# The conditioning product of a two-layer kernel in 64-row tiles of the array, in place of a block-diagonal matrix

## The reference, cut to what matters

```
x = x + L0_ffn(L0_cond(x))      # L0_cond: out[b,d,t] = sum_c x[b,c,t] * W[cond[b]][c,d], W is 64 x 64
x = x + L1_ffn(L1_cond(x))
```

## Time and profile before

| | us |
|---|---|
| runs | 2144.24, 2148.28, 2148.89 (median 2148.28) |
| span of the profiled execution | 2146.3 |
| TensorE matmul busy | 2024.6 (94%) |
| TensorE weight load busy | 1896.7 (88%) |
| VectorE busy | 1691.0 (79%) |
| GpSimd busy | 554.9 (26%) |
| ScalarE busy | 488.7 (23%) |
| L947 matmuls (conditioning product) | 1024, median 275 ns |
| L964 / L965 / L966 matmuls | 1536 each, mean 342 / 341 / 341 ns |

### The profile page before, as it was taken

The page is one execution under the profiler, slowest core; times in us unless marked ns, Lnnn a source line. Parts: engine busy times, 40 slices in busy tenths (PEclk is TensorE's granted clock), DMA queues, the critical chain, the costliest instruction groups (busy, mean ns, idle before and its releaser), DMA issues.

```text
span 2146.3 us, 37287 instructions
## 1 busy us (share of the span) xinstructions
PE 2024.6 (94%) x11969; PEld 1896.7 (88%) x12032; DVE 1691.0 (79%) x4631; ACT 488.7 (23%) x1312; POOL 554.9 (26%) x470
## 2 busy tenths in 40 slices
PE   7989899999999999999999999999999999999997
PEld 6989899999999999999988788878887888888885
DVE  6898886555555555555579999999999999999999
ACT  3111111111111111111123322232223222322232
POOL 3644311111111111111123232233223332323222
PEclk9999999999999999999999999999999999999999
DMA  7754433233233332332444444444444444444442
GB/s 241 239 154 134 124 115 115 90 109 101 90 112 98 98 111 90 110 100 90 145 126 134 134 125 148 133 134 125 149 132 125 134 129 148 128 134 131 146 129 81
DMA packets 152577, 273.07 MB, mean 127 GB/s; under 512 B 30179, under 2 KB 101861, under 8 KB 152550
## 3 DMA queue, kind: packets, MB, share of 16 engines
q1 hardware_dynamic: 152550, 272.77, 41.6%
HBM read 163.62 MB, written 109.05 MB: 127 GB/s over the span
## 4 chain that ended last, share of the span: by engine, by line
PE 49%; DVE 43%; issue 5%; ACT 1%; SPq 1%; DMA 1%; DVEq 0%; ACTq 0%
PE bank_g L964 11%; PE bank_g L966 11%; PE bank_g L965 11%; DVE rounded L858 8%; DVE rqt L346 6%; PE bank_t L947 4%; DVE ht L327 4%; DVE obuf L888 3%; DVE val L856 3%; DVE rq_blocks L870 3%; DVE st_l L878 2%; PE bank_g L1018 2%; PE bank_g L1017 2%; PE bank_g L1016 2%; PE bank_f L1027 2%
## 5 line engine op out<-in xcount | busy, mean ns | idle before, releaser
L964 PE MATMUL bank_g<-w0h,st_h 128*128 128x384 f32 (+1 forms) x1536 | 524.9, 342 | 20.5 <-DVE x1buf L824 17.4
L966 PE MATMUL bank_g<-w0h,st_l 128*128 128x384 f32 (+1 forms) x1536 | 523.4, 341 | 0.0
L965 PE MATMUL bank_g<-w0l,st_h 128*128 128x384 f32 (+1 forms) x1536 | 523.1, 341 | 0.0
L1016 PE MATMUL bank_g<-w1h,st_h 128*128 128x352 f32 x1536 | 506.3, 330 | 2.9 <-DVE st_l L878 2.5
L1018 PE MATMUL bank_g<-w1h,st_l 128*128 128x352 f32 x1536 | 496.3, 323 | 0.0
L1017 PE MATMUL bank_g<-w1l,st_h 128*128 128x352 f32 x1536 | 496.1, 323 | 0.0
L553 POOL TENSOR_TENSOR xbuf<-xbuf,b_base_sb 128x1024 f32<-128x1024 f32 x64 | 153.7, 2402 | 707.0 <-PE bank_t L947 693.0
L964 PEld LDWEIGHTS bank_g<-w0h,st_h 128*128 128x128 f32 x1536 | 291.1, 190 | 23.8 <-DVE st_l L723 19.1
L1016 PEld LDWEIGHTS bank_g<-w1h,st_h 128*128 128x128 f32 x1536 | 289.1, 188 | 10.8 <-DVE st_l L878 3.5
L966 PEld LDWEIGHTS bank_g<-w0h,st_l 128*128 128x128 f32 x1536 | 291.2, 190 | 0.0
L965 PEld LDWEIGHTS bank_g<-w0l,st_h 128*128 128x128 f32 x1536 | 291.0, 189 | 0.0
(11 more groups left out here) (84 smaller groups left out, 2384.7 us busy)
## 6 DMA issues: line engine op xcount, KB each, us to landing
xbuf<-x SPq DMA_DIRECT2D x64, 512.0 KB, 4.0
x_scratch<-x1buf SPq DMA_DIRECT2D x64, 512.0 KB, 2.9
x1t_scratch<-x_blocks SPq DMA_DIRECT2D x256, 128.0 KB, 2.3
xbuf<-x1t_scratch SPq DMA_DIRECT2D x64, 512.0 KB, 3.7
x1buf<-x_scratch SPq DMA_DIRECT2D x64, 512.0 KB, 5.1
out<-obuf SPq DMA_DIRECT2D x64, 512.0 KB, 2.7
b_stack<-b_split SPq DMA_DIRECT2D x384, 64.0 KB, 3.3
raw<-a_split SPq DMA_DIRECT2D x128, 128.0 KB, 4.2
```

The costliest lines, as they stand in the source:

```text
L964: pe.matmul(to, st_h[:, rows], w0h[:, k, cols], start=(k == 0), stop=False)
L965: pe.matmul(to, st_h[:, rows], w0l[:, k, cols], start=False, stop=False)
L966: last = pe.matmul(to, st_l[:, rows], w0h[:, k, cols], start=False, stop=(k == KC - 1))
L1016: pe.matmul(to, st_h[:, rows], w1h_k[:, k, cols], start=(k == 0), stop=False)
```

## The change

The conditioning product no longer uses a 128 x 128 matrix with zeros. `wpair` holds the two 64 x 64 matrices under one another, 128 rows x 64 columns, without clearing. Each block k becomes two products, j = 0 and 1, each with 64 rows of `xbuf` (64 x 128, stationary) and 64 rows of `wpair` (64 x 64, moving). They write to different banks: `bank_t` and `bank_f` become views of one tensor `bank_c` of four banks, and half h of batch j goes to bank 2h + j, 4 x 64 columns of it. ScalarE's copy and VectorE's subtraction keep their number and size, and read two banks each (`turned_half`) and write or read the operand in the matching order (`as_turned`). The memset of the matrix, its semaphore and SyncE's wait for it go away.

```diff
-        bank_t = whole.enter_context(nc.psum_tensor("bank_t", [P, 2, 512], F32))
-        bank_f = whole.enter_context(nc.psum_tensor("bank_f", [P, 2, 512], F32))
+        bank_c = whole.enter_context(nc.psum_tensor("bank_c", [P, 4, 512], F32))
+        bank_t, bank_f = bank_c[:, 0:2, :], bank_c[:, 2:4, :]
...
-            wbd = sb("wbd", [P, 2, P], F32, p1)
+            wpair = sb("wpair", [P, 2, CH], F32, p1)
...
+            def turned_half(h):
+
+                return bank_c[:, 2 * h:2 * h + 2, 0:HALF // 2].rearrange("p j (k d) -> p j k d", d=CH)
+
+            def as_turned(operand, h):
+
+                part = operand[:, h * HALF:(h + 1) * HALF]
+                return part.rearrange("p (k j d) -> p j k d", j=PER_TILE, d=CH)
...
-                sp.wait_ge(wbd_zeroed, 1)
-
...
-                        sp.dma_start(wbd[rows, b, rows],
+                        sp.dma_start(wpair[rows, b, :],
...
-                pool.memset(wbd[:, :, :], 0.0).then_inc(wbd_zeroed, 1)
...
-                        act.activation(st_h[:, h * HALF:(h + 1) * HALF], bank_t[:, h, :], ACT.Copy)\
-                           .then_inc(hi_done[h], 1)
+                        act.activation(as_turned(st_h, h), turned_half(h), ACT.Copy).then_inc(hi_done[h], 1)
...
-                    half = slice(h * HALF, (h + 1) * HALF)
                     dve.wait_ge(hi_done[h], t + 1)
-                    dve.tensor_tensor(st_l[:, half], bank_t[:, h, :], st_h[:, half], ALU.subtract)\
+                    dve.tensor_tensor(as_turned(st_l, h), turned_half(h), as_turned(st_h, h), ALU.subtract)\
...
-                        cols = slice((k % 4) * P, (k % 4 + 1) * P)
-                        last = pe.matmul(bank_t[:, k // 4, cols], xbuf[:, b, k * P:(k + 1) * P], wbd[:, b, :],
-                                         start=True, stop=True)
+                        cols = slice((k % 4) * CH, (k % 4 + 1) * CH)
+                        for j in range(PER_TILE):
+                            rows = slice(j * CH, (j + 1) * CH)
+                            last = pe.matmul(bank_c[:, 2 * (k // 4) + j, cols], xbuf[rows, b, k * P:(k + 1) * P],
+                                             wpair[rows, b, :], start=True, stop=True)
```

More of the change, by code:

```diff
@@ L173, in build @@
             b_base_loaded = sem("b_base_loaded")
-            wbd_zeroed = sem("wbd_zeroed")
             st_ps = [sem(f"st_ps{h}") for h in range(2)]
```

## The result

| | median, us | runs | ratio to before (95% interval) |
|---|---|---|---|
| before, beside it | 2148.59 | 4 | |
| changed kernel | 2168.24 (2166.43 to 2168.91) | 4 | 1.0093 (1.0078 to 1.0107) |
| predicted | 2165 (2138 to 2292) | | |

The change costs 19.7 us. The profiled execution has a span of 2166.4 us.

The account below looks back on a forecast made before the run. TensorE was taken to bound nearly all 64 first-layer tiles, L947 being worth 114 us. The terms 0 + 17 + 0 + 0 = +17 us on 2148.3 gave 2165 us, range 2138 to 2292.

Parts of the forecast that it names:

- early waits: Six TensorE waits before 270 us for the operand's lower halves, about 19 us, while VectorE also quantizes a weight.
- Item 1: L947's pairs of load and matmul go from 16 to 32 a tile, row halves side by side: taken as 0 us.
- Item 2: The array changes to 64-row tiles and back: 0 to 0.54 us a tile, middle taken, 17 us.
- running empty: At each change of tile size the array must empty before the next load: 0.17 us.
- uncovered load: At each change of tile size the next load can't hide behind the last matmul: 0.11 us.
- sum by full tolls: Every change of tile size pays its toll in full: 2148 + 34 = 2182 us.
- Items 3 to 6: Second half's first load, two-bank reads by ScalarE and VectorE, dropped memset, unchanged GpSimd and ScalarE waits: each taken as 0.
- likeliest case: L947's loads lie side by side, changes of tile size cost 17 us: 2165 us, own range 2145 to 2189, chance 0.50.
- rival A: L947's loads of the two row halves queue up, 32 steps a tile: 2244 to 2295 us, chance 0.34.
- Rival B: In L947 the stream, not the load, sets the step, which falls to 58 ns: -54 us, 2094 us, chance 0.16.
- What the profile would show: Signs: L947's loads in pairs every 110 ns, its block 1.7 to 2.3 us long, the tile's period 16.16 us.

Follow-up runs that it names:

- half stream: The kernel before, still in 128-row tiles, with 64 moving columns in place of 128 in the conditioning product: 2146.3 us, ratio 0.9989.
- 64-row pair of experiment 1: The kernel before with one of a tile's eight products done a second time, in two 64-row tiles, into banks nobody reads: 2184.5 us, ratio 1.0169.
- run with one half first: The changed kernel with all eight products of the first row half ahead of all eight of the second: 2265.3 us, ratio 1.0557.

## Why the prediction was right, step by step

*What bounds the kernel.* Right. The change moved the period of every steady tile by its own cost. Apart from the early waits nothing else moved.

*Item 1, the pieces.* Right: side by side, 16 steps of 111 ns, 0 us. The argument from the earlier trace rows, that the load and not the stream sets the step and that fewer rows don't shorten it, is confirmed by the half stream and by the 111 ns of 64-row loads. The argument from the earlier trace rows, that a load passes a matmul that still waits, led to the right end but told only half: a load also passes other loads, of the other row half, and not more than about three of them.

*Item 2, the toll.* The mechanism was right, the size off: I took the middle of 0 and 0.54 us a tile, 0.27, and it is 0.34. The term that was mis-sized is running empty, for which I took 0.17 us from the time a matmul is still busy after its successor has started. At the entry the load starts 0.27 us after the last 384-column matmul, and a successor would have gone after 0.18, so it is 0.09. The uncovered load costs its 0.11 as taken. The 64-row pair of experiment 1 has a 128-column matmul ahead of its entry, at 716.47 in this row:

```profile
716.47 0.28 PE L947 MATMUL bank_t<-wbd,xbuf 128*128 128x128 f32 x1
```

The load starts at 716.68, 0.21 us later; less the 0.11 after which a successor would have gone, that is 0.10. So the emptying hardly depends on the length of the matmul ahead. At the exit the whole toll is 0.15 us. If the last matmuls wait for their loads and then stream for 0.05 us, 0.10 of it is emptying again; that they do is assumed, as their rows don't date the stream. Taking neither end was a choice without a row behind it, and it was luck that the middle lay near. The time came nearer than the toll: 22 us by the periods where 17 were taken, less what sank into the early waits.

*The rule that a change of tiling mode drains TensorE* (the Trainium skill, TensorEngine Tiling (Array Packing), section Key Properties). The traces agree: a delay of 0.20 us at each entry, put down to no semaphore, one of 0.15 us at each exit, beside which no releaser stands, and none between one row half and the other. The sum by full tolls, 2182, was too high: the toll is 0.34 us a tile and not the 0.54 that I had worked out.

*Items 3 to 6.* The second half's first load starts within 0.01 us of the first, nothing. ScalarE's copy is at 598 ns (597), so the 0.03 us of L664 did not come, and VectorE's subtraction is at 681: nothing. The early waits shrank by 2.6 us, which the likeliest case did not count and rival A did.

*Rival A* fell for this order of the products. The run with one half first comes nearest to it, with 27 steps of 31, at 2265 us, of which 25 are the lower clock; the price of 2244 to 2295 had no term for the clock. The reasons given for it were wrong. The order of the parts within a product lies inside the window. And a load does not wait until the one before it is through: in the earlier trace rows the load of 24.77 lasts until 24.96, and the next starts at 24.88. What holds is the distance of 0.11 us between their starts.

*Rival B* fell with the half stream: no change where it wanted -54 us. *The promise of up to 2x* (the Trainium skill, TensorEngine Tiling (Array Packing), section Theoretical Speedup) doesn't come about in this trace for row tiles alone, where each load keeps its 128 columns: 16 steps of 111 ns, 1.78 us, before and after. With the columns cut as well, the steps fall from 1.78 to 0.94 us, near the 2x, and the toll takes nearly half of the gain.

*What the profile would show.* Pairs of loads every 110 ns: yes. A block of 1.7 to 2.3 us: 1.93. A period of 16.16: 16.23.

## What to carry to other kernels

Ask of a short matmul which half of it sets the step, the load of the stationary operand or the stream: here the load set it, and cutting the rows and the moving operand gained nothing as long as the load kept its columns. Cut the columns of the load too (here the gain came with both cut), and alternate the tiles of the array within a few pieces. And count the switches of tile size, 0.34 us here for the way in and out together: a block must save more than that, so a few long blocks are worth more than many short ones. When a run comes out longer than its period says, look at the granted clock by stretch before looking for another cause.

## What the runs showed of the hardware that was not expected

- A 4-byte load of 128 columns keeps its successor waiting 111 ns, at 128 or 64 rows alike; one of 64 columns (64 rows, with a stream of 64 columns) at most 59 ns.
- Four 64 x 64 tiles load side by side: four loads are through within 0.15 us of the first one's start.
- A load of the other row half was taken about three loads ahead of its turn, in both orders tried, and no further.
- A switch from 128-row to 64-row tiles costs 0.20 us and the way back 0.15 us, and the sum was the same 0.34 us with 4 pieces in between and with 32.
- The granted clock fell to 1.2 GHz behind some of the blocks of 3.32 us in which loads come mostly singly, and cost 1.56 us each time; behind blocks of 1.93 or 2.54 us it did not fall between 270 and 1040 us.
- A longer tile can cost nothing, and a shorter one gain less than its period, in a stretch where another engine sets the pace: waits on the lower halves went from 16.5 to 3.0 us with 0.36 us more a tile, and from 16.5 to 25.3 us with 0.8 us less.
